# Cross attention with split fp32 products: context dots in two gaps per value tile, and a new order of loads, stores and x splits between value loop and first batch

## The reference

```python
# q = x (16,512,512); k = v = ctx (16,77,512); D = 512
qp = q @ Wq + bq;  kp = k @ Wk + bk;  vp = v @ Wv + bv
w = softmax(einsum('bqd,bkd->bqk', qp, kp) / sqrt(512))
x = einsum('bqk,bkd->bqd', w, vp)
gate = concatenate((qp, x), axis=-1) @ Wg + bg
x = x * mask[..., None] * sigmoid(gate)
return x + q
```

## Time and profile before

| | |
|---|---|
| device time, median of 3 runs | 458.12 us (457.96 to 458.17) |
| the profiled execution's own time | 457.82 us |
| its span | 456.0 us |
| PE busy | 416.3 us (91%) |
| DVE busy | 218.0 us (48%) |
| ACT busy | 151.8 us (33%) |
| POOL busy | 129.3 us (28%) |
| mean share of the DMA engines | 60.5% |
| mean granted PE clock | 0.979 of full |

### The profile page before, as it was taken

How to read it: one execution, slowest core, us unless ns; L and a number is a source line. 1 busy time by engine, 2 the same in 40 slices (tenths; PEclk the granted TensorE clock), 3 DMA queues, 4 the chain that set the end, 5 groups by cost and what they waited for, 6 DMA issues and landing times.

```text
span 456.0 us, 5307 instructions
## 1 busy us (share of the span) xinstructions
PE 416.3 (91%) x1928; PEld 334.7 (73%) x1928; DVE 218.0 (48%) x384; ACT 151.8 (33%) x283; POOL 129.3 (28%) x98
## 2 busy tenths in 40 slices
PE   4999978789938099999999999999999999999996
PEld 3879966568726078788787787877878778787784
DVE  3685566653303034535355354462554634536344
ACT  4544232222231314144242341432414424143221
POOL 0005064344361304042240431404404134041200
PEclk9999999999979789999999999999999999999999
DMA  7974424335941864775857858668576685676412
GB/s 240 389 274 186 136 79 184 137 134 162 368 157 48 236 195 145 239 204 210 280 172 227 246 182 256 184 225 261 172 240 194 213 265 183 227 205 224 154 46 92
DMA packets 43125, 90.86 MB, mean 199 GB/s; under 512 B 5276, under 2 KB 5276, under 8 KB 42460
## 3 DMA queue, kind: packets, MB, share of 16 engines
q1 hardware_dynamic: 43100, 90.53, 60.5%
HBM read 63.51 MB, written 27.00 MB: 198 GB/s over the span
## 4 chain that ended last, share of the span: by engine, by line
PE 81%; DMA 5%; DVE 4%; POOL 3%; SPq 2%; issue 2%; ACT 1%; DVEq 0%; ACTq 0%
PE bank L394 38%; PE bank L306 26%; PE bank L417 3%; PE bank L418 3%; PE bank L424 3%; PE bank L425 3%; DMA v_dram<-v_st 3%; DVE dot_tmp L560 2%; DMA x_raw<-in_xT 2%; PE bank L407 1%; PE bank L404 1%; POOL wg L705 1%; POOL xT L705 1%; POOL v_st L705 1%; SPq L243 1%
## 5 line engine op out<-in xcount | busy, mean ns | idle before, releaser
L394 PE MATMUL bank<-wqg,xT 128*128 128x512 f32 x768 | 192.3, 396 | 0.0
L394 PEld LDWEIGHTS bank<-wqg,xT 128*128 128x128 f32 x768 | 143.1, 190 | 29.6
L705 POOL TENSOR_TENSOR xT<-x_raw,xT 128x512 fp32r<-128x512 f32 x64 | 87.9, 1403 | 199.3 <-ACT xT L458 199.3
L668 DVE SCALAR_TENSOR_TENSOR prod_sb<-tanh_sb,bank 128x512 f32<-128x512 f32 x64 | 43.9, 686 | 131.7 <-ACT tanh_sb L528 115.6
L528 ACT ACTIVATE tanh_sb<-bank 128x512 f32<-128x512 f32 x64 | 38.4, 600 | 126.5 <-PE bank L418 126.5
L306 PE MATMUL bank<-xT,mt 128*77 128x512 f32 x192 | 49.1, 406 | 7.3 <-POOL xT L705 7.3
L679 DVE SCALAR_TENSOR_TENSOR out_sb<-prod_sb,half_mask,x_rows 128x512 f32<-128x512 f32 x64 | 48.0, 750 | 1.7
L306 PEld LDWEIGHTS bank<-xT,mt 128*77 128x77 f32 x192 | 29.0, 151 | 24.2 <-POOL xT L705 7.5
L458 ACT ACTIVATE xT<-x_raw 128x512 fp32r<-128x512 f32 x64 | 35.2, 617 | 10.2 <-DMA x_raw<-in_xT 10.2
L306 PE MATMUL bank<-wg,vT 128*128 128x512 f32 (+1 forms) x120 | 29.5, 394 | 7.3 <-DVE vT L555 7.3
L417 PE MATMUL bank<-v_ext,wT 122*128 122x512 f32 x64 | 25.7, 402 | 11.1 <-ACT wT L539 11.1
(11 more groups left out here) (72 smaller groups left out, 378.7 us busy)
## 6 DMA issues: line engine op xcount, KB each, us to landing
x_raw<-in_xT SPq DMA_DIRECT2D x64, 256.0 KB, 5.5
x_rows<-in_x SPq DMA_DIRECT2D x64, 256.0 KB, 3.9
out_y<-out_sb SPq DMA_DIRECT2D x64, 256.0 KB, 2.1
v_ext<-v_dram SPq DMA_DIRECT2D x32, 308.0 KB
v_dram<-v_st SPq DMA_DIRECT2D x18, 512.0 KB, 3.0
v_ext<-v_dram SPq DMA_DIRECT2D x16, 180.0 KB
ctxT_raw<-in_ctxT SPq DMA_DIRECT2D x4, 624.0 KB, 8.6
ctx_rows<-in_ctx SPq DMA_DIRECT2D x4, 616.0 KB
```

Source lines behind the costliest of these rows:

```text
L394: pe.matmul(gate_ps[n % 3][:, :], xT[b % 2][:, s, c, q], wqg[:, m, c, :], start=(c == 0 and (s, m) == PRODUCTS[0]), stop=False)
L668: dve.scalar_tensor_tensor(prod_sb[:, n % 2, :], tanh_sb[:, n % 2, :], 1.0, attn_ps[n % 2][:, :], ALU.add, ALU.mult).then_inc(prod_made, 1)
L705: pool.tensor_tensor(dst, src, f32(hi_), ALU.subtract).then_inc(made, 1)
```

## The change

DVE: the 16 context dots, formerly up to three at the end of each of steps 0 to 5 of the value loop, are now two in each of steps 1 to 8, one between vT LO and `v_f`, one between `v_f` and `vg_f`. Their order is 12 to 15, then 0 to 11. `sb_c` is made at step 9 (before: 6). `add_sb(0)` stands ahead of `vg_f(9)` (before: behind it).

SP: x_raw(0) is loaded in two halves at k = 5 and 6, rows of x(0) at k = 7 and 8, x_raw(1) right after the loop's last step, then v_ext(0) and v_ext(1) behind a wait for the stores of tiles 0 and 1 only, then the last store, the rows of x(1), and then the wait for all stores.

ACT and POOL: xT(0) is split at k = 7 (before: 9), each ahead of its own work for `vg(6)`.

```diff
+SB_ORDER = [12, 13, 14, 15] + list(range(12))
@@ SP
-            for k in range(KT + 1):
-                if k < KT:
-                    store_v(k)
-                if k >= 1:
-                    store_vg(k - 1)
-                if k == 6:
-                    sync.wait_ge(dots_made, DOT["sb", B - 1] + 1)
-                    load_xT(0)
-                    for b in range(2):
-                        for t in range(T):
-                            load_rows(b, t)
-            for i in range(2):
-                sync.wait_ge(v_stored[i], 16 * ((KT + 1 - i) // 2))
-                sync.wait_ge(vg_stored[i], 16 * ((KT + 1 - i) // 2))
-            sync.wait_ge(job_done, J["v", KT - 1] + 1)
-            load_vext(0)
+            for k in range(KT):
+                store_v(k)
+                if k >= 1:
+                    store_vg(k - 1)
+                if k == 5:
+                    sync.wait_ge(dots_made, DOT["sb", 3] + 1)
+                    load_xT(0, (0, 1))
+                if k == 6:
+                    load_xT(0, (2, 3))
+                if k == 7:
+                    sync.wait_ge(dots_made, DOT["sb", 7] + 1)
+                    load_rows(0, 0)
+                    load_rows(0, 1)
+                if k == 8:
+                    load_rows(0, 2)
+                    load_rows(0, 3)
             sync.wait_ge(xT_lo, C)
             load_xT(1)
+            sync.wait_ge(job_done, J["v", KT - 1] + 1)
+            wait_stored(2)
+            load_vext(0)
+            load_vext(1)
+            store_vg(KT - 1)
+            sync.wait_ge(dots_made, DOT["sb", 11] + 1)
+            for t in range(T):
+                load_rows(1, t)
+            wait_stored(KT)
             for b in range(B):
-                if b + 1 < B:
-                    if b >= 1:
-                        sync.wait_ge(attn_done, b * T)
+                if 1 <= b < B - 1:
+                    sync.wait_ge(attn_done, b * T)
                     load_vext(b + 1)
@@ ACT (POOL alike, with xT_lo_of(0))
-                if k == KT - 1:
-                    act.wait_ge(dots_made, DOT["sb", B - 1] + 1)
+                if k == 7:
+                    act.wait_ge(dots_made, DOT["sb", 15] + 1)
                     act.wait_ge(wg2_lo, C)
                     xT_hi_of(0)
@@ DVE, value loop
+                if 1 <= k <= B // 2:
+                    ctx_dot(SB_ORDER[2 * k - 2])
                 if k < KT:
...
                     dve.tensor_tensor(v_f[0:n, :], ...)
+                if 1 <= k <= B // 2:
+                    ctx_dot(SB_ORDER[2 * k - 1])
+                if k == KT:
+                    add_sb(0)
                 if k >= 1:
...
                     dve.tensor_tensor(vg_f[0:n, :], ...)
-                for b in range(3 * k, min(3 * k + 3, B)):
-                    ctx_dot(b)
-                if k == 6:
-                    dve.wait_ge(dots_made, DOT["sb", B - 1] + 1)
+                if k == KT - 1:
+                    dve.wait_ge(dots_made, DOT["sb", SB_ORDER[-1]] + 1)
                     dve.tensor_scalar(sb_c[:, :], ...)
@@ DVE, ahead of the batch loop
-            add_sb(0)
             softmax_max(0)
```

## The result

The changed kernel takes 435.81 us (434.56 to 437.48) against 458.14 for the kernel before; the ratio is 0.951 (0.947 to 0.955). It is faster by 22 us, where 30 were forecast (428.3), and lies above the range of 426.0 to 434.0. The profiled execution took 435.96 us, with a span of 434.2.

The account below looks back on a forecast made before the run. PE was taken to lose time only between 62 and 166 us, to dots, late transfers and a lowered clock. Gains 1.5 + 7.0 - 1.5 + 11.1 + 9.6 + 2.1 = 29.8 us gave 428.3, range 426.0 to 434.0.

Parts of the forecast that it names:

- Step 1: Value loop, dots moved to new places on DVE: 7.04 us gained over five periods, 1.47 at vg(0).
- Rival (b): Value loop: each tile's first dot is on PE's path through the exclusion with POOL; 434.9 us, chance 0.06.
- Rival (e): Value loop: dots were not the cause, vT HI on ACT takes their place; 7.0 us missing, 435.3, chance 0.03.
- Step 2: Split of xT(0) at k = 7: chunk 3 lands in 4.0 us, PE loses 1.5 (0.5 to 3.0), no clock loss.
- Step 3: vg(8) to turn_scores(0): 8.7 us instead of 19.81, 11.1 gained, 1.5 of it from add_sb.
- Step 4: turn_scores(0) to attend(0,0): 9.6 us gained of 18.0, leaving 8.4 with a 0.8 wait for v_ext(0).
- Step 5: attend(0,0) to scores_T(1): 4.63 us instead of 6.73 with the clock no longer down, 2.1 gained.
- rival (c): One wait, for v_ext(0) or x_raw(1), grows past 5 us and slow matmuls follow; 436.7 us, chance 0.04.
- rival (a): Transfers land later (chunk 3 at 5.5, v_ext(0) or x_raw(1) at 8.4), POOL costs 1.0; 431.7 us, chance 0.23.

Follow-up runs that it names:

- c0: The changed kernel timed again with no edit: 437.59 us, ratio 0.955 to the kernel before.
- e3: Changed kernel with v_ext(1) loaded only after the last store, the rows of x(1) and the wait for all stores: 437.03 us.
- e6: Changed kernel with the dots part undone: three dots behind vg_f in steps 1 to 5, one in step 6, new batch order kept: 444.31 us.
- e1: Changed kernel with all four x_raw chunks of batch 0 loaded at k = 5, split still at k = 7: 432.91 us.
- e9: Changed kernel, SP reordered: x_raw(0) whole at k = 5, x_raw(1) at k = 8, v_ext(0) at k = 9, other loads behind the last store: 427.62 us.
- e2: Changed kernel with ACT and POOL splitting xT(0) at k = 8 instead of 7, loads unchanged: 434.45 us.
- e13: Changed kernel with two sets of 12 unread matmuls, ahead of PE's waits for vT LO(7) and ahead of attend(0,0): 434.12 us.
- e7: Changed kernel with the add_sb(0) part undone, so it stands behind vg_f(9) again: 434.60 us.
- e8: Changed kernel where SP, behind v_ext(0) and the last store, waits for v_ext(0) to land before loading v_ext(1) and rows of x(1): 434.45 us.
- e4: Changed kernel with each 77-row copy into v_ext issued as one of 64 rows and one of 13: 437.13 us.
- e5: Changed kernel with v_ext(0) issued ahead of x_raw(1) instead of behind it: 437.95 us.
- e11: Changed kernel with v_ext(0) issued at k = 9 once PE has done v(9), ahead of the last stores and x_raw(1): 438.21 us.
- e10: The early-loads kernel e9, with ACT and POOL also splitting xT(1) in the value loop's last step: 428.39 us.

## Why the prediction was wrong, and where it was right

Against its own timeline the profiled execution is 8.0 us late (435.96 against 428.0). Steps 2, 4 and 5 failed: two landing times were taken too short, and the slow clock behind the two gaps was put at nothing. In order of time:

- Start: v(1) at 63.37 instead of 62.69, 0.7 us. This is scatter, not the change: with the same code up to there, c0 has 63.45, e3 62.68.
- Step 1, the dots: 7.04 and 1.47 us, right to 0.1 (five periods of 29.80; vg(0) 2.86 after v(1), forecast 2.87). Rival (b) is excluded. Undone in e6 the dots cost 6.7. Rival (e) fell with it. The full blocking that speaks against k = 8 was there to see (the second dot took 1.15 us there) and had 2 us of room; where gap 1 is gone, it costs 0.9 us ahead of vg(8) (e1, e9).
- Step 2, the split: mis-sized twice. The landing was taken as 4.0 us "near the lower rows" and was 5.6, so the gap is 3.05, the value written down for the upper bound, not 1.5. The nearest row was not used: the same chunks at the same k = 6 had landed in 5.7 to 6.0 in the kernel before. And "no clock loss" was read off from waits of 1.3 us, while the gap at hand could be 3.0 by the same paragraph: vg(7) took 1.5 us more. Together 3.1 to 3.3 us too little. e1 and e2 show the landing as the cause, e13 the clock.
- Step 3: right, 8.61 us from vg(8) to turn_scores(0), forecast 8.7. But 1.5 of it, add_sb(0), bought nothing, since gap 2 ended by a transfer (e7). In the forecast that wait was 0.8 us, so part of this was to be seen even there.
- Step 4: 11.03 us instead of 8.4. The landing of v_ext(0) was taken as 7.5 with 8.4 as the upper bound, and was 9.4; that is 1.9 of the 2.6 us. The rest is its last issue, 1.5 us after turn_scores(0) instead of 0.9. The bound came from one row with 8.06. That "every landing beside other traffic in this stretch was 8 us" was misread: in the trace before, among and behind the twelve x loads, chunks landed in 5.7 to 6.0 us, rows of x in 6.2 to 7.5, and stores in 7.5 to 9.0. The change crowds the same queue in another place: 4.9 MB are issued between 124 and 135 us, and the windows from 130 us on move 264 to 349 GB/s. An estimate from these numbers, 14 to 19 us for all of it, says that the queue stays full past the time when v_ext(0) is wanted, and so that a wait must be expected; it does not give its length, since only about 3.5 MB had moved when v_ext(0) landed at 138.2.
- Step 5: 6.22 instead of 4.63, 1.6 us of slow clock behind gap 2. The place for it was rival (c), whose "past 5 us" came from a window with the clock at 0.93 in the third gap; here it fell after 2.7 and 3.6 us, and in e7 behind a gap of 2.12.

The cause was thus rival (a), late transfers, and its size rival (c)'s clock on top. They were weighed as if they excluded each other (431.7 and 436.7); in truth the first brings the second, and the measured time lies between.

Left open: why the second pair of chunks takes 5.6 us and the first 4.0 with the same stores beside them (it is no scatter: 5.2 to 5.9 against 3.7 to 4.3 in eleven profiles), what makes v_ext(0) take 8 us even in e8, and why the clock did not fall in e3's profiled execution after 3.32 us without work, when it fell in c0's after 2.89 and in e7's after 2.12.

## What to carry to other kernels

When waits for data go away, add up the bytes that the new order puts in flight between two points and divide by the rate that full windows show. If that is longer than the time until the data are wanted, expect a wait; its length stays uncertain, since that rate was 230 GB/s in one full stretch and 391 in another (e4). A landing time taken from another traffic is no bound; one of the same transfer at the same place is the better guess (5.7 to 6.0 against 5.6). Order loads by when they are needed and let those with the latest need go last (e9: 10 us from four moved lines), and move all that share the full stretch, since moving one alone hands the wait to the next (e5, e11). A wait of 2 to 4 us on PE can cost 1.4 to 2.9 us more in slow matmuls behind it; where it can't be removed, matmuls that nobody reads may cover it (e13: 1.7 to 3.5 us). And where POOL is given work at a new place, look for DVE instructions on the path beside it (e10).

## What the runs showed of the hardware

- The granted clock fell to half 2.7 and 3.6 us after PE had run dry in the changed kernel's profile and about 5 us in the profile before. The shortest wait that it fell behind was 2.12 us (e7); behind one of 3.32 us it did not fall in one execution (e3). With 24 extra matmuls in the gaps it stayed at 1.00 in three of four executions and at 0.998 in the fourth (e13). How long it then stays at half differs too: 4.29 us for vg(7) in c0, 5.46 in e11, behind waits of 2.89 and 3.21.
- A landing depends on what is issued behind it: v_ext(0) took 9.4 us with 2.4 MB behind it (8.7 to 10.5 in other profiles) and 8.0 with 0.4 MB (e8). x_raw(1) took up to 10.0 with v_ext(1) right behind it (e11), 5.5 to 6.6 when issued at k = 8, some 10 us earlier (e9).
- The Trainium skill, "DMA: Bandwidth & Descriptors", Why a DMA increments its semaphore by 16 and not by 1, would have copies of 77 rows use 11 engines. No row names the engines of a copy, but the share agrees: 0.68 of 16 engines with v_ext(0) and the last store on their way (e8), 0.72 at 277 GB/s toward the end of the changed kernel's full stretch, and 1.04 at 391 GB/s at the same time with copies of 64 and 13 rows (e4); 11 of 16 is 0.69. It brought no time, since the full stretch moved no more bytes.
- A DVE instruction that reads two tiles in SBUF and a POOL subtraction hold each other up: dots of 1.82 and 1.17 us beside POOL instead of 0.8 and 0.7, and POOL's splits 5.50 instead of 4.93 (e1). The cast of w_a, which reads one tile, took 1.27 us instead of 0.32 beside POOL (e10).
